# A relational graph layer on one core: the first tile of x loaded in two halves, another order of the first six turns, and the watch three groups behind instead of five

## What is computed

```python
h = jnp.maximum(_layernorm(x, axis=-1), 0.0)
# rel 1 (loop), with adj transposed:
p = h @ W_loop.T
g = p @ Wg_loop.T
vals = (p + b_loop) * jax.nn.sigmoid(g + bg_loop)
x = x + jax.nn.relu((adj_t == 1) @ vals)
```

## Time and profile before

| | |
|---|---|
| median of 3 runs | 105.48 us (104.98 to 105.68) |
| the profiled execution | 104.91 us, of which 103.1 us are the span of its instructions |
| busy | PE 95.1 us, DVE 90.1, ACT 89.2, POOL 85.4 |
| TensorE's granted clock | full in every slice of the span |
| DMA | 25.45 MB, 247 GB/s on average |

### The profile page before, as it was taken

One profiled execution on the slowest core, in us unless ns is written; L12 is line 12 of the kernel. 1 busy time (PEld: TensorE's weight loads), 2 busy tenths in 40 slices (PEclk: granted clock), 3 DMA queues, 4 the chain that ended last, 5 costly groups with the idle time before them and its releaser, 6 DMA issues.

```text
span 103.1 us, 2492 instructions
## 1 busy us (share of the span) xinstructions
PE 95.1 (92%) x802; PEld 90.8 (88%) x802; DVE 90.1 (87%) x196; ACT 89.2 (87%) x145; POOL 85.4 (83%) x161
## 2 busy tenths in 40 slices
PE   5966899998999999999999999999999999999920
PEld 2645789797999999999999999999999999999920
DVE  2289989999999999999999999999999596867841
ACT  4165498895799998999899989998999899999990
POOL 2278999999999999999999999999999999960000
PEclk9999999999999999999999999999999999999999
DMA  2899999999999999999999999999943323425192
GB/s 68 246 302 295 293 290 290 290 296 291 274 306 289 326 308 327 283 316 320 336 316 336 318 333 314 338 299 309 304 133 96 116 87 95 115 63 147 35 283 88
DMA packets 50272, 25.45 MB, mean 247 GB/s; under 512 B 850, under 2 KB 50260, under 8 KB 50260
## 3 DMA queue, kind: packets, MB, share of 16 engines
q1 hardware_dynamic: 49984, 25.17, 87.5%
q10 hardware_dynamic: 276, 0.13, 0.4%
HBM read 16.91 MB, written 8.39 MB: 245 GB/s over the span
## 4 chain that ended last, share of the span: by engine, by line
PE 70%; POOL 4%; ACT 4%; issue 1%; DVE 0%; POOLq 0%
PE psum L784 22%; PE psum L762 12%; PE psum L763 12%; PE psum L767 12%; PE psum L749 11%; ACT junk L439 3%; POOL rstd L336 3%; POOL xn L349 1%; ACT gate L433 0%; PE psum L809 0%; DVE dist_sum L626 0%; DVE flag L628 0%; POOLq L359 0%
## 5 line engine op out<-in xcount | busy, mean ns | idle before, releaser
L349 POOL TENSOR_SCALAR xn<-x_all,mean_neg,rstd 128x128 f32<-128x128 f32 x101 | 44.8, 456 | 0.7 <-POOL rstd L336 0.4
L762 PE MATMUL psum<-w_hi,hT_hi 128*128 128x256 f32 x128 | 33.8, 299 | 1.2 <-DVE w_lo L587 0.8
L784 PE MATMUL psum<-vals,mask 128*128 128x128 f32 x256 | 33.6, 275 | 0.1
L418 ACT ACTIVATE psum<-bias_all 128x1024 f32<-128x1024 f32 x32 | 33.1, 1035 | 0.3 <-DVE vals L555 0.3
L784 PEld LDWEIGHTS psum<-vals,mask 128*128 128x128 f32 x256 | 31.0, 191 | 0.2 <-issue 0.2
L763 PE MATMUL psum<-w_lo,hT_hi 128*128 128x256 f32 x128 | 31.0, 277 | 0.0
L522 DVE BATCH_NORM_STATS2 stats<-x_all 128x6 f32<-128x256 f32 x64 | 23.9, 418 | 3.3 <-DMA x_all<-in_x 3.1
L762 PEld LDWEIGHTS psum<-w_hi,hT_hi 128*128 128x128 f32 x128 | 24.1, 188 | 2.0 <-DVE w_lo L587 1.1
L555 DVE TENSOR_TENSOR vals<-psum,gate 128x512 f32<-128x512 f32 (+1 forms) x33 | 21.9, 664 | 4.0 <-ACT gate L433 3.2
L336 POOL TENSOR_TENSOR rstd<-var_eps,minus_half 128x16 f32<-128x16 f32 (+2 forms) x11 | 24.5, 2223 | 0.1
L763 PEld LDWEIGHTS psum<-w_lo,hT_hi 128*128 128x128 f32 x128 | 24.2, 189 | 0.0
(11 more groups left out here) (36 smaller groups left out, 30.9 us busy)
## 6 DMA issues: line engine op xcount, KB each, us to landing
adj_all<-in_adj SPq DMA_DIRECT2D x16, 512.0 KB, 6.9
x_all<-in_x SPq DMA_DIRECT2D x15, 512.0 KB, 7.2
out<-x_all SPq DMA_DIRECT2D x15, 512.0 KB, 6.0
x_all<-in_x SPq DMA_DIRECT2D x2, 256.0 KB, 3.0
out<-x_all SPq DMA_DIRECT2D x1, 256.0 KB, 2.4
out<-x_all ACTq DMA_DIRECT2D x1, 128.0 KB, 2.5
out<-x_all SPq DMA_DIRECT2D x1, 128.0 KB, 2.6
w_raw<-in_L_gnn_W_loop SPq DMA_DIRECT2D x1, 64.0 KB, 2.3
```

Of the source, the lines that this page charges most:

```text
L349: last = pool.tensor_scalar(xn[:, g % XN, j * D:j * D + D], x_all[:, g * GC + j * D:g * GC + j * D + D], mean_neg[:, b % BATCH_SLOTS, k:k ...
L418: nc.scalar.activation(prod_ps[s].rearrange("p g a d -> p g (a d)"), bias_all[:, :, :].rearrange("p a d -> p (a d)").unsqueeze(1) .to_broa ...
L762: nc.tensor.matmul(to, hi, w_hi[:, :], start=False, stop=False, skip_group_check=True)
L784: last = nc.tensor.matmul(to[:, j * D:j * D + D], mask[:, g % MASKS, j * N:j * N + N], vals[:, s, j * D:j * D + D], start=True, stop=True)
```

## The change

- SP loads the first tile in two halves (graphs 0 and 1 on a new semaphore x_half, graphs 2 and 3 on x_first), then the second tile, and only then the two weights. adj's chunk 0 comes ahead of x's chunk 3.
- VectorE: `row_stats(0)` waits for each half before its own bn_stats. The order of the first turns is written anew, up to turn 3 instead of turn 1, and the loop starts at 4.
- ScalarE: the first turns in another order, with the masks of groups 0 to 3 and the seed and relu of group 3 among them; its loop starts at 2.
- GpSimd's share of group 6 is 2 graphs instead of 3, VectorE's 2 instead of 1.
- WATCH_LAG 3 instead of 5: `watch(0)` comes at turn 3. Two calls stand behind the last gate, where three stood. The store that ScalarE issues stays behind the second of them.
- The mask of group 28 goes from ScalarE to GpSimd (LAST_MASK_ACT).
- TensorE gets five more products of zeros ahead of its wait for the weights.

```diff
--- before.py
+++ after.py
@@ -34,10 +34,12 @@
     BATCHES = [(0, 0), (1, 1), (2, 3), (4, 5)] + [(g, min(g + 3, GROUPS - 1)) for g in range(6, GROUPS, 4)]
     BATCH = 4 * GROUP
 
-    POOL_SHARES = (0, 4, 4, 0, 4, 4)
+    POOL_SHARES = (0, 4, 4, 0, 4, 4, 2)
 
     BATCH_SHARES = (3, 4, 3, 3)
-    WATCH_LAG = 5
+    WATCH_LAG = 3
+
+    LAST_MASK_ACT = GROUPS - 4
 
     ctx = ExitStack()
     with ctx:
@@ -88,6 +90,7 @@
 
         x_loaded = [sem(f"x_loaded{n}") for n in range(CHUNKS)]
         adj_loaded = [sem(f"adj_loaded{n}") for n in range(CHUNKS)]
+        x_half = sem("x_half")
         x_first = sem("x_first")
         w_loaded = sem("w_loaded")
         bias_cleared = sem("bias_cleared")
@@ -222,7 +225,7 @@
             return sum(any(pool_share(g) for g in range(BATCHES[k][0], BATCHES[k][1] + 1)) for k in range(b))
 
         def mask_by_act(g):
-            return g < 4 or g % MASKS == 0
+            return g < 4 or g % MASKS == 0 and g < LAST_MASK_ACT
 
         def masks_before(g, by_act):
             return sum(mask_by_act(k) == by_act for k in range(g))
@@ -254,14 +257,15 @@
             def load_adj(c):
                 load_tile(adj_all, adj, c * CG, c * CC, CG, adj_loaded[c])
 
-            load_tile(x_all, x, 0, 0, GROUP, x_first)
+            load_tile(x_all, x, 0, 0, GROUP // 2, x_half)
+            load_tile(x_all, x, GROUP // 2, GC // 2, GROUP - GROUP // 2, x_first)
+            load_tile(x_all, x, GROUP, GC, CG - GROUP, x_loaded[0])
             sp.dma_start(w_raw[:, 0, :], W_loop).then_inc(w_loaded, 16)
             sp.dma_start(w_raw[:, 1, :], Wg_loop).then_inc(w_loaded, 16)
-            load_tile(x_all, x, GROUP, GC, CG - GROUP, x_loaded[0])
             load_x(1)
             load_x(2)
+            load_adj(0)
             load_x(3)
-            load_adj(0)
             for c in range(4, LOAD_AHEAD):
                 load_x(c)
                 load_adj(c - 3)
@@ -457,12 +461,16 @@
             relu_turned(1)
             edges(0)
             seed(2)
+            sigmoid(1)
             relu_turned(2)
-            sigmoid(1)
             edges(1)
+            seed(3)
+            relu_turned(3)
+            sigmoid(2)
             edges(2)
+            edges(3)
             act.wait_ge(half_ready, 1)
-            for t in range(1, GROUPS - 1):
+            for t in range(2, GROUPS - 1):
                 if live(t + 2):
                     relu_turned(t + 2)
                     seed(t + 2)
@@ -472,14 +480,13 @@
                 if live(t + 2) and mask_by_act(t + 2):
                     edges(t + 2)
                 if t == GROUPS - 2:
-                    watch(CHUNKS - 3)
-            watch(CHUNKS - 2)
+                    watch(CHUNKS - 2)
+            watch(CHUNKS - 1)
             act.wait_ge(half_out, 1)
             act.dma_start(
                 out[B - GROUP:B - GROUP // 2, :, :].rearrange("b n d -> n b d"),
                 x_all[:, (B - GROUP) * D:(B - GROUP // 2) * D].rearrange("p (b d) -> p b d", b=GROUP // 2)
             ).then_inc(stored, 16)
-            watch(CHUNKS - 1)
 
 
             act.wait_ge(flag_ready, 1)
@@ -511,7 +518,7 @@
 
                 b, first, final = batch_of(g)
                 if g == 0:
-                    dve.wait_ge(x_first, 16)
+                    dve.wait_ge(x_half, 16)
                 elif g % CHUNK == 0 or g == 1:
                     dve.wait_ge(x_loaded[g // CHUNK], 16)
                 if g == first and b >= BATCH_SLOTS:
@@ -519,6 +526,8 @@
                     dve.wait_ge(rstd_ready, b - BATCH_SLOTS + 1)
                     dve.wait_ge(mean_ready, means_before(b - BATCH_SLOTS + 1))
                 for j in range(0, GROUP, 2):
+                    if g == 0 and j >= GROUP // 2:
+                        dve.wait_ge(x_first, 16)
                     last = nc.vector.bn_stats(
                         stats[:, b % BATCH_SLOTS, ((g - first) * GROUP + j) // 2, :],
                         x_all[:, g * GC + j * D:g * GC + (j + 2) * D].rearrange("p (b d) -> p d b", b=2))
@@ -593,24 +602,33 @@
             normalise(0)
             split_weights(0)
             row_stats(2)
+            split_weights(1)
             row_stats(3)
-            split_weights(1)
             low_part(0)
             row_stats(4)
             row_stats(5)
-            row_stats(6)
             messages(0)
             low_part(1)
+            normalise(3)
+            row_stats(6)
+            messages(1)
             row_stats(7)
-            normalise(3)
             low_part(2)
-            messages(1)
+            output(0)
             row_stats(8)
-            output(0)
             low_part(3)
+            output(1)
             row_stats(9)
+            messages(2)
             row_stats(10)
-            for t in range(2, GROUPS + 1):
+            low_part(4)
+            row_stats(11)
+            messages(3)
+            output(2)
+            normalise(6)
+            low_part(5)
+            row_stats(12)
+            for t in range(4, GROUPS + 1):
                 if live(t):
                     messages(t)
                 output(t - 1)
@@ -732,6 +750,7 @@
             pe.wait_ge(bias_loaded, 32)
             nc.tensor.matmul(bank[7][:, 256:512], ones[:, :], bias_row[:, :, :].rearrange("p a d -> p (a d)"),
                              start=True, stop=True).then_inc(bias_spread, 1)
+            keep_busy(5, 1)
             pe.wait_ge(ident_step, 2)
             pe.wait_ge(w_loaded, 32)
             turn_weights(w_raw[:, 0, :], w_raw[:, 1, :], w_gT[:, :], w_turned, w_gT_ready, 1, 3)
```

## The result

The changed kernel takes 104.4 us (median of 13 runs, 104.12 to 105.2), the kernel before 105.22 us (13 runs, 104.98 to 106.68). The ratio is 0.9931, with a 95% interval of 0.9904 to 0.9958: 0.7 us faster, or 0.8 us by the medians. (A median counts every execution; ratios and intervals leave out the few that took over 1.5% more than the fastest of their kernel.) The forecast was 1.74 us. The median lies within the range of 102.9 to 104.9 us, but more than half of the gain that was forecast is missing, and nearly all of what came comes from the kernel's end. The profiled execution took 104.12 us with a span of 102.3 us, against 104.91 and 103.1.

The account below looks back on a forecast made before the run. GpSimd was taken to set the pace from the head on, with the flag and last store deciding the end. Head 0.94 plus end 0.8 made 1.74 us, so 105.48 - 1.74 = 103.7 us, range 102.9 to 104.9.

Parts of the forecast that it names:

- The bound: GpSimd's unbroken work from 6.31 us sets the pace, 10.87 us per four groups; a gain at group 6 stays.
- the extra watch in the loop and of the mask of group 28: ScalarE's 14th watch call inside the loop and a mask moved to GpSimd: cost nothing, bounds 0 and 0.3 us lost.
- The second tile: Load of graphs 4 to 7, issued third: there at 4.75, 0.70 us sooner; GpSimd's coefficients of batch 1 gain 0.65 us.
- Chunk 1 of x: Load that VectorE's statistics of group 2 wait for: issued 0.5 us later but left at 7.55, bounds 7.3 and 8.0.
- VectorE's order: VectorE's new order from 7.55 reaches group 9's statistics at 19.00, so GpSimd's batch 4 starts at 19.18, 0.56 us sooner.
- rival 1: Head: the early tile buys little, VectorE's chain to group 9 starting late; 0.1 instead of 0.56, 104.2 us; chance 0.17.
- The exchange of adj and x: adj's first chunk and x's chunk 3 change places among the loads: no gain counted, x's chunk 3 there at 12.95.
- rival 5: Slower: x's chunk 3 behind adj comes late for VectorE's group 6, each microsecond past 13.28 costing one; chance 0.04.
- The column of group 6: Two columns on GpSimd instead of three: saves 0.43 less 0.05 us for overlap with VectorE; group 6 turned at 23.8.
- The end: Behind the last gate: flag 1.13 us sooner, last store still lands at 101.8, closing 0.5; gain 0.8, bounds 0.3 and 1.13.
- The weights: Loads of w issued later: TensorE begins turning at 5.64 instead of 4.68; VectorE keeps 0.55 us of cover.
- both together: The early tile buys little and the last stores keep the end: 0.78 us in all, 104.7 us; chance 0.08.

Follow-up runs that it names:

- the end alone: The kernel before with only the watch brought forward (lag 3, one call fewer behind the last gate, mask of group 28 on GpSimd): 104.89 us against 105.78, ratio 0.9929.
- group 9 first: The changed kernel with the statistics of group 9 ahead of output 1 on VectorE: 104.39 us, ratio 0.9881; a second time 104.26 us, ratio 0.9879.

## Why the prediction was wrong

**The bound: right.** GpSimd paced the kernel from batch 4 on. The cycles are 10.87 us in both. Of the 0.08 us gained at the turn of group 6, 0.03 are left near the end (the last aggregate starts at 97.59 instead of 97.62). The seventeen profiles together show it best: the turn of group 6 lies anywhere from 24.36 to 26.08 us in them, and the last gate follows it by 72.0 to 72.6 us in every one. The same distance, 72.24 us in the changed kernel and 72.19 before, shows no cost of the extra watch in the loop and of the mask of group 28 beyond that scatter, as forecast.

**The second tile: right.** Read at 4.87 for 4.75, coefficients of batch 1 at 5.72 for 5.65.

**Chunk 1 of x: this is the step that failed.** The prediction said: "with as many bytes ahead of it as before; I leave it at 7.55, bounds 7.3 and 8.0". It came at 8.15, and at 7.97 and 8.27 in the other two profiles of the changed kernel. That is 0.4 to 0.7 us, and with it went all that batch 1 had won, since no statistics means no coefficients of batch 2.

Two things were wrong. The loads of the kernel before land the chunk at 7.53 in one profile and at 7.86 in another (the end alone), and 7.55 was taken as its time. And the same bytes ahead do not mean the same landing. Windows of GpSimd as in the earlier trace rows, whose last two numbers are the busy share of the DMA engines and their GB/s, before and then in the changed kernel:

```profile
4.00:6.00 2.00, 1.23 (x2) 1.00 1.06 317
```

```profile
4.00:6.00 2.00, 1.43 (x4) 1.00 0.67 192
```

In the changed kernel the transfers ahead of the chunk ran out before its own were moving, and the engines stood partly idle. It is so in all eleven profiles with the changed kernel's loads ahead of the chunk: shares of 0.52 to 0.80, and the chunk lands at 7.85 to 8.55 (on average over its 16 parts at 7.14 to 7.78). With the loads of before the shares are 1.06 and 1.08, and the parts land at 6.88 and 7.08 on average; with the weights on ScalarE, where SP issues the chunk at 2.26, it is 1.00 and 6.88.

Why they ran out is argued: the chunk is issued at 3.27 instead of 2.72, behind two issues of 0.5 us that bring 64 KB each, where before the 256 KB of the second tile stood right ahead of it. The halves are the one issue more. Taking them back (chunk issued at 2.84) was worth 0.35 us alone and 0.4 us beside group 9 first (103.86 against 104.26), neither clear of the scatter by itself. The gap is smaller in one of these profiles (0.85, landing at 7.69) and not in the other (0.62, landing at 8.48). What the halves alone cost is thus supported by times, not settled by landings.

**VectorE's order: the second step that failed.** Its chain from group 2 to the result of group 9 was summed to 11.53 us and took 19.96 - 8.15 = 11.81. Two terms were short: the four columns of group 3 took 1.16 us, not 1.02, beside GpSimd's, and messages 0 waited 0.2 us for the gate. The text saw that the chain "has no room between it and GpSimd" and made it rival 1 at 0.17; with chunk 1 late, it had to be the forecast. Batch 4 came 0.31 us later than before instead of 0.56 sooner, 0.87 us off: 0.60 from chunk 1 and the rest from the chain.

**The exchange of adj and x.** It was put at nothing, with only a danger in it (rival 5). The run without it lost 0.8 us: the new order needs the mask earlier than the old one did.

**The column of group 6: right in this profile, not as a fixed price.** 0.38 us were forecast; the turn follows the coefficients by 4.61 us instead of 5.00, so 0.39, and 0.44 between the two kernels that differ in it alone. In six other profiles, one of the changed kernel among them, it is only 0.2 to 0.3 us, because one GpSimd column beside VectorE's two takes 0.74 to 0.76 us instead of 0.58.
The Trainium skill (SBUF — State Buffer, section "SBUF: two separate sides") states a lock by which the loser fully blocks, and on VectorE's side it ties it to a two-port mode or two inputs in SBUF; the traces do not show the mode. By the prediction's working of that rule the column would have saved 0.1. No profile has so little: some are near the forecast, and six lie between the two.

**The end: right in size, not in its working.** 0.8 us were forecast; 0.75 came (0.78 in the span, less the 0.03 from ahead). I let the flag's way gain 1.13 and the stores cut it to 0.8, with 0.5 us of closing. The closing takes 0.4, so the stores would have allowed 0.9; what cut the gain is the load of the flag, 0.37 us longer while the stores move. Two errors of opposite sign, so the size was partly luck.

**The weights** came 0.8 us later than forecast on TensorE (6.44 for 5.64) and held VectorE for 0.61 us, but that wait lay ahead of one for chunk 1.

Put together: 0.03 and 0.75 instead of 0.94 and 0.8. The case "both together" had the total (0.78 us) at a chance of 0.08, for a head of 0.48 and an end of 0.3, so it was near for another reason.

## What to carry to other kernels

A load that is brought forward counts until the next load that the same engine needs: follow each of them through the list of issues, ask whether the DMA engines still have work when it is issued, and take no landing time from one execution as the time (here the same load was read 0.4 us apart in two profiles of the same loads). Where an order written by hand puts work that waits for another engine ahead of work that the pacing engine waits for, move the latter first; here one line, and one DMA issue fewer in the head, made 103.86 us of 104.76. At the end of a kernel, look at every way that ends late: here the last store's would have allowed an end only 0.2 us sooner, so a flag 0.8 us sooner than the changed kernel's moved the end by little.

## What the runs showed of the hardware

A register load of one number from SBUF took 0.46 us on SP when the DMA engines were nearly idle (share 0.00 to 0.03) and 0.83 to 0.92 us while stores moved, 1.03 us once; without the last stores it was back at 0.46. I had not expected an instruction of that size to depend on traffic. Whether it is the traffic or something else of those stores that slows it was not tried.

The 16 parts of one load do not land together. For chunk 1 the first and the last part were 0.9 us apart in the kernel before and 1.4 us in the changed one, and between 0.95 and 1.9 us in the other profiles. In the changed kernel's profile it is 1.4 us for the next loads too, so the late parts are late once and stay so. VectorE waits for the last part, so this scatter goes straight into the head. What makes one part late stays open; it was not tried.
